# A graph network's filter layer: one-hots compared with a row of numbers in PSUM, place sums read in neighbouring order

## The reference

```python
h = x @ w_in + b_in
Wij = ssp(f_ij @ w_f1 + b_f1) @ w_f2 + b_f2      # ssp = softplus - log 2
Wij = Wij * rcut_ij[:, None]                     # one row of 64 per edge
x_ij = h[idx_j] * Wij
agg = jax.ops.segment_sum(x_ij, idx_i, num_segments=n_atoms)
out = ssp(agg @ w_o1 + b_o1) @ w_o2 + b_o2
```

## Time and profile before

| what | us |
|---|---|
| median of 3 runs | 7495.95 |
| lowest and highest | 7493.87, 7500.98 |
| the profiled execution | 7511.49 |
| its span in the profile | 7509.8 |

### The profile page before, as it was taken

One profiled execution on the slowest core, in us unless ns is written; L12 is line 12 of the kernel. 1 busy time (PEld: TensorE's weight loads), 2 busy tenths in 40 slices (PEclk: granted clock), 3 DMA queues, 4 the chain that ended last, 5 costly groups with the idle time before them and its releaser, 6 DMA issues. The chain is left out here.

```text
span 7509.8 us, 155131 instructions
## 1 busy us (share of the span) xinstructions
PE 5888.8 (78%) x41800; PEld 4261.6 (57%) x41800; DVE 5381.3 (72%) x14198; ACT 3602.2 (48%) x5657; POOL 5249.8 (70%) x5375
## 2 busy tenths in 40 slices
PE   7777777777777888878777774666999999999994
PEld 6555555555555666666555553554666666666662
DVE  7766767677677888888888884445777777777774
ACT  2555555555555555555555552044333333333334
POOL 4677777777777777777777775534777777777770
PEclk5666666666666667676667776677999999999995
DMA  4222222111113333333333335744222222222222
GB/s 127 79 83 82 84 84 69 55 56 54 55 55 89 111 114 115 110 118 94 93 96 93 93 89 157 248 133 152 77 76 76 77 77 77 76 76 76 76 77 74
DMA packets 512098, 695.12 MB, mean 93 GB/s; under 512 B 255299, under 2 KB 367645, under 8 KB 510879
## 3 DMA queue, kind: packets, MB, share of 16 engines
q1 hardware_dynamic: 317008, 347.69, 16.3%
q0 software_dynamic: 181376, 321.40, 14.5%
q10 hardware_dynamic: 13498, 24.07, 1.0%
HBM read 450.80 MB, written 241.85 MB: 92 GB/s over the span
## 5 line engine op out<-in xcount | busy, mean ns | idle before, releaser
L1688 POOL DMA_INDIRECT msg_tab<-big x3224 | 3318.4, 1029 | 1076.3 <-issue 1076.0
L2239 POOL DMA_INDIRECT big<-y_parts,big x1616 | 1589.2, 983 | 547.7 <-issue 485.5
L2320 ACT CAST big<-ps 128x980 bf16<-128x980 f32 x804 | 783.9, 975 | 1272.3 <-PE ps L2268 1269.6
L2280 PE MATMUL ps<-big 128*128 128x384 bf16 x6566 | 1196.4, 326 | 0.2 <-ACT big L2320 0.2
L2372 DVE TENSOR_SCALAR big<-big,dstF 128x343 bf16<-128x343 f16 (+2 forms) x3216 | 981.9, 338 | 238.5 <-PE ps L2268 235.5
L1187 PEld LDWEIGHTS ps<-big 128*128 128x128 f32 x3224 | 651.4, 300 | 432.9 <-ACT big L1376 432.9
L1187 PE MATMUL ps<-big 128*128 128x128 f32 x3224 | 764.0, 412 | 154.6 <-ACT big L1376 154.6
L1381 ACT CAST big<-big 128x512 bf16<-128x512 f32 x403 | 249.2, 618 | 1213.4 <-DMA msg_tab<-big 1213.0
L1491 DVE TENSOR_TENSOR big<-big 128x512 f32<-128x512 f32 x403 | 279.2, 693 | 762.6 <-ACT big L1381 759.9
L2280 PEld LDWEIGHTS ps<-big 128*128 128x128 bf16 x6566 | 580.5, 97 | 347.9 <-issue 1.0
L1487 DVE TENSOR_REDUCE big<-big 128x8 f32<-128x784 f32 x403 | 637.7, 1582 | 13.7
(11 more groups left out here) (289 smaller groups left out, 10740.7 us busy)
## 6 DMA issues: line engine op xcount, KB each, us to landing
arena<-msg_tab SPq DMA_DIRECT2D x97, 727.5 KB, 4.6
big<-msg_tab SPq DMA_DIRECT2D x97, 630.5 KB, 4.1
big<-in_edge_attr SPq DMA_DIRECT2D x403, 128.0 KB
msg_tab<-big POOLq DMA_INDIRECT x3224
big<-msg_tab SPq DMA_DIRECT2D x97, 388.0 KB, 3.4
msg_tab<-big SPq DMA_DIRECT2D x97, 291.0 KB
big<-y_parts,big POOLq DMA_INDIRECT x1616
big<-h_parts SPq DMA_DIRECT2D x403, 48.0 KB
```

The source lines that it names most:

```text
L1688: nc.gpsimd.indirect_dma_start(out=m.msg_tab[:, :], out_offset=bass.IndirectOffsetOnAxis(ap=sidx[s][:, j:j + 1], axis=0), in_=row[s][:, j, ...
L2239: nc.gpsimd.indirect_dma_start(out=m.grow[s][:, 3 * D * j:3 * D * j + 3 * D], out_offset=None, in_=m.y_parts[:, :], in_offset=bass.Indirec ...
L2280: mm = pe.matmul(ps_rows, m.cnt[h][:, a, :], m.y_part[:, HALF * h + a, :], start=(h == 0 and a == 0), stop=(h == 1 and a == HALF - 1))
L2320: nc.scalar.copy(m.cnt[h][:, :, SLOTS * i:SLOTS * i + SLOTS].rearrange("p h (a w) -> p h a w", a=2), ps_cnt[i % 2][:, :, 0:SIDE * HALF].re ...
```

## The change

- The bf16 table `digit` goes. Instead VectorE copies the numbers 0 to 127 once as fp32 into PSUM (`ps_count`, in the bank that also holds `ps_rank`), and L1477 compares against that row, each number repeated by a step of zero.
- `hot_seg`'s compare (L1531) reads `ps_count` too, instead of `node_early`. It moves from the end of the stage to right behind L1477, ahead of the sum L1481.
- `prod` now lies edge by edge (p, j, h): L1485 writes at a step of 98 words, L1487 reads neighbouring words.
- The wait for `total_made` moves ahead of the first compare, since PE writes `ps_rank` in the same bank; PE waits for the tables before it zeroes `ps_rank`.

```diff
@@ -860,8 +860,7 @@
     row = [v.bitcast(BF16).rearrange("p (j c) -> p j c", j=J) for v in slots(8176, J * MROW // 2)]
     far = work[:, 9728:10240].bitcast(BF16)
     tile_hot = m.spare[:, 0:NBK]
-    prod = work[:, 10240:10240 + NBK * J].rearrange("p (h j) -> p h j", j=J)
-    digit = work[:, 11024:11024 + NBK * J // 2].bitcast(BF16).rearrange("p (h j) -> p h j", j=J)
+    prod = work[:, 10240:10240 + NBK * J].rearrange("p (j h) -> p j h", j=J)
     lower = work[:, 11416:11544]
     sidx = [v.bitcast(U32) for v in slots(11544, J)]
     rank = slots(11560, J)
@@ -921,6 +920,7 @@
     ps_row = ps[:, 3, :]
     ps_rank = ps[:, 4, 0:NBK]
     ps_attr = ps[:, 5, 0:2 * P]
+    ps_count = ps[:, 4, P:2 * P]
     ps_dst = ps[:, 6:8, :].rearrange("p a b -> p (a b)")
     ps_bucket = [ps[:, t, 0:3 * F] for t in range(3)]
     e_ps_attr = ps[:, 1, 0:2 * P]
@@ -1249,8 +1249,8 @@
             pe.sem_inc(total_made, 1)
             pe.sem_inc(deg_turned, 2)
             pe.sem_inc(bucket_summed, 3)
+            pe.wait_ge(tables_put, 4)
             pe.matmul(ps_rank, m.zeros[0:1, 0:P], m.zeros[0:1, 0:NBK], start=True, stop=False, skip_group_check=True)
-            pe.wait_ge(tables_put, 4)
             pe.sem_inc(seg_summed, 1)
             staged_parts(pe, G, stage)
 
@@ -1458,7 +1458,7 @@
             dve.wait_ge(weighed_done, ready(g, 1))
 
         def dve_windows(dve):
-            nc.vector.tensor_copy(digit, m.iota_w[:, 0:NBK].unsqueeze(2).to_broadcast([P, NBK, J])).then_inc(tables_put, 1)
+            nc.vector.tensor_copy(ps_count, m.iota_w[:, :]).then_inc(tables_put, 1)
             nc.vector.tensor_scalar(lower, m.below[:, :], -1.0, 1.0, ALU.mult, ALU.add).then_inc(tables_put, 1)
             for s in range(2):
                 nc.vector.memset(row[s][:, :, MROW - 1:MROW], 0.0).then_inc(tables_put, 1)
@@ -1473,18 +1473,20 @@
                 dve.wait_ge(low_done, free(g))
                 nc.vector.tensor_tensor(msg, ps_row, weighed, ALU.mult).then_inc(msg_done, 1)
 
-            def rank_hots(g):
-                nc.vector.tensor_tensor(hot, digit, m.hi16[:, bass.ds(g * J, J)].unsqueeze(1).to_broadcast([P, NBK, J]),
+            def rank_hots(g, part):
+                dve.wait_ge(total_made, free(g))
+                nc.vector.tensor_tensor(hot, ps_count[:, 0:NBK].unsqueeze(2).to_broadcast([P, NBK, J]), m.hi16[:, bass.ds(g * J, J)].unsqueeze(1).to_broadcast([P, NBK, J]),
                                         ALU.is_equal).then_inc(hot_done, 1)
+                if part and not (isinstance(part[1], int) and part[1] == NBK - 1):
+                    hot_seg(*part)
                 dve.wait_ge(hot_done, ready(g, 0))
-                dve.wait_ge(total_made, free(g))
                 nc.vector.tensor_reduce(tile_hot, hot, AX.X, ALU.add).then_inc(hots_added, 1)
 
             def ranks(g, s):
                 dve.wait_ge(prefix_made, ready(g, 0))
-                nc.vector.tensor_tensor(prod, hot, ps_rank.unsqueeze(2).to_broadcast([P, NBK, J]), ALU.mult).then_inc(rank_mul, 1)
+                nc.vector.tensor_tensor(prod.rearrange("p j h -> p h j"), hot, ps_rank.unsqueeze(2).to_broadcast([P, NBK, J]), ALU.mult).then_inc(rank_mul, 1)
                 dve.wait_ge(rank_mul, ready(g, 0))
-                nc.vector.tensor_reduce(rank[s], prod.rearrange("p h j -> p j h"), AX.X, ALU.add).then_inc(rank_done, 1)
+                nc.vector.tensor_reduce(rank[s], prod, AX.X, ALU.add).then_inc(rank_done, 1)
 
             def rest(g, s):
                 dve.wait_ge(high_done, ready(g, 0))
@@ -1528,7 +1530,8 @@
                 nc.vector.tensor_copy(seg_low[:, 0:n], seg[s][:, 0:n, 3 * F]).then_inc(seg_lows, 1)
                 dve.wait_ge(seg_lows, q + 1)
                 dve.wait_ge(seg_summed, q + 1)
-                nc.vector.tensor_tensor(seg_hot[:, 0:P * n].rearrange("p (n r) -> p n r", r=n), node_early[:, :, 0:n],
+                nc.vector.tensor_tensor(seg_hot[:, 0:P * n].rearrange("p (n r) -> p n r", r=n),
+                                        ps_count.unsqueeze(2).to_broadcast([P, P, n]),
                                         seg_low[:, 0:n].unsqueeze(1).to_broadcast([P, P, n]), ALU.is_equal).then_inc(seg_hots, 1)
 
             def seg_loads(phase, s, k):
@@ -1541,7 +1544,7 @@
                 if before:
                     message(*before[:2])
                 if here:
-                    rank_hots(here[0])
+                    rank_hots(here[0], (*part, slot_of(part, here)) if part else None)
                 if part and not (isinstance(part[1], int) and part[1] == 0):
                     fold_seg(part[0], part[1] - 1, slot_of(part, here) ^ 1)
                 if before:
@@ -1554,8 +1557,6 @@
                     places(*before[:2])
                 if after:
                     dve_hidden(dve, after[0], hid[after[1]], relu, log1p)
-                if part and not (isinstance(part[1], int) and part[1] == NBK - 1):
-                    hot_seg(part[0], part[1], slot_of(part, here))
             for t in range(2):
                 dve.sem_inc(parts_out[t], 16)
             dve.sem_inc(seg_folded, 1)
```

## The result

The kernel with the change takes 7525.53 us (median of 6 runs, 7518.53 to 7531.95), the kernel before 7498.47 us (6 runs, 7482.70 to 7503.00): a ratio of 1.0038, 95% interval 1.0025 to 1.0051. It is slower by some 27 us, where 38 were forecast. The profiled execution took 7525.14 us, its span 7523.4 us. The spans differ by only 13.6 us (7509.8 before), since the profiled execution of before lay 13 us above the median of its runs and that of after on its median.

What follows compares the result with a forecast made beforehand. In the first band VectorE's 10.29 us barely exceeds GpSimd's bare 10.15, and whichever has more to do sets the turn. First band +36 us, second +2, without buckets 0: +38 us, median 7534 us, 8-in-10 range 7450 to 7590.

Steps and rivals of the forecast that it cites:

- The side: Whole kernel: slower, chance 0.60, against 0.20 for the same and 0.20 for faster.
- VectorE's sum sets the first band: First band with buckets: VectorE's turn becomes 10.29 + 0.41 + 0.79 - 0.01 = 11.48 us, over 11.11 us.
- Every price of an instruction: VectorE: place compare about 0.96 us, node compare 1.9 and 1.2, product 1.55, sum over buckets 0.97.
- The two halves of the sums cancel: L1485 and L1487: sum -0.61 us by neighbouring reads, product +0.60 by its strided store, together -0.01 us.
- The turns without buckets hide all of it: Turns without buckets: VectorE's 3.1 us of slack hide +0.40 us, so 0.
- the strided store: L1485's store at 98 words: +0.60 us taken, bounds 0 and +0.61; the quoted skill figure would give 1.14 us.
- First band: The 98 turns of the first band with buckets: +0.37 us each, +36 us in all.
- Nothing on the path gains by that … Both cost nothing: Moved node compare and wait for total_made: PE's 3.85 us of idle goes, but both were priced at nothing.
- Second band: The 97 turns of the second band: VectorE 10.81 us against 10.86; 0 to +0.1 us taken, +2 us in all.
- GpSimd's own time stays near 10.8 as well, since the stretches at L1498 stay: Second band: GpSimd's turn not shortened by the change, the ground for taking 0 to +0.1 us.
- GpSimd is freed: Rival, L1531 and L1477: without two SBUF operands their stretches end, both bands 10.65 us, -65 us, 7431 us; chance 0.07.
- GpSimd meets L1498: Rival, turns without buckets: L1498 over about 0.1 us earlier stretches a DMA instruction, +80 us, about 7610 us; chance 0.10.

Runs made afterwards that it cites:

- old_sums: The changed kernel with prod back in its old order, dense product store and strided sum over buckets: 7524.58 us, ratio to before 1.0028.
- node_sbuf: The changed kernel with the node compare reading the old bf16 table in SBUF again, at its new place: 7441.12 us, ratio to before 0.9920.
- no_move: The changed kernel with the node one-hot back at the end of VectorE's stage, plus a wait for total_made: 7613.14 us, ratio to before 1.0160.
- move_only: The kernel before with only the node one-hot moved behind the place one-hot, both tables in SBUF: 7464.89 us, ratio to before 0.9952.
- place_psum: The kernel before with only the place compare changed to read the row in PSUM: 7474.34 us, ratio to before 0.9982.
- place_row_sbuf: The kernel with the bf16 node compare (node_sbuf), its place compare reading the fp32 row from SBUF instead of PSUM: 7506.56 us, ratio to before 1.0021.
- row_in_sbuf: The changed kernel with both compares reading the same fp32 row from SBUF instead of PSUM: 7552.35 us, ratio to before 1.0081.
- sum_later: The kernel before with the sum over buckets L1487 moved behind the low part L1498: 7574.76 us, ratio to before 1.0108.
- low_first: The kernel before with L1495 (0.2 us) moved behind L1498, which so comes about 0.1 us earlier: 7526.97 us, ratio to before 1.0034.
- hidden_later: node_sbuf with the hidden sum L1452 moved into the next stage, between L1456 and L1474: 7424.91 us, ratio to before 0.9911.
- hidden_move: move_only with the hidden sum L1452 moved between L1456 and L1474: 7487.41 us, ratio to before 0.9999.

## Why the prediction was right, and where not

**Right, and shown.** The side: slower, by 27 us where 38 were forecast, 7525.5 us in the forecast's own range. VectorE's sum sets the first band: 11.48 us forecast, 11.43 on the timeline, with GpSimd behind L1505. Every price of an instruction: 0.96, 1.9 and 1.2, 1.55, and 0.97 us were forecast for what took 0.963, 1.891, 1.224, 1.575 and 0.970. The two halves of the sums cancel (old_sums). The turns without buckets hide all of it (10.65 and 10.63). And the repeated fp32 row is what costs: node_sbuf gets 84 us back by a bf16 table.

On the strided store the trace stood nearer to my bounds than to the figure I had quoted. The product went from 966 to 1575 ns, 0.78 ns an element. The 1.14 us estimated from the Trainium skill's 24-word step (Vector Engine (DVE) Microarchitecture Reference, "Measured stream behaviour on trn2") did not come; the same table has 1.75 ns a column for reads at 72 and 152 words, and that is the row which the 98-word store is like, with 1.044 + 0.78 = 1.82.

**First band, mis-sized: +25 us for +36.** The steady turn was near the forecast. From one of GpSimd's pauses to the next 14 turns take 11.41 us each, and the last four turns of the band only 10.53, 10.50, 10.48 and 10.18: VectorE starts its last compare of 1664 elements at 3441 us, 40 us before GpSimd is through with the band. So 11.37 us is the mean. The sum took the steady turn for all 98.

**The step that failed: "Nothing on the path gains by that … Both cost nothing".** The move is worth 40 us by itself, and undoing it in the change costs 88, of which some 40 are the old place and 48 the wait in the shared bank. The sum had nothing for it. I took two turns of the timeline in which VectorE waits for nothing as the band. The row of L1485 in the earlier trace rows has 49.2 us of waiting for PE's L1212, and 44.9 of these lie in 45 turns of the first band. They belong to a loop: node one-hot last on VectorE, 3.85 us of PE idle, counts late, VectorE late. Where VectorE sets the pace, as in the change, such a wait adds to the turn (0.34 us in no_move). In the kernel before GpSimd sets it, and there the move pays by GpSimd's stretch, 0.82 to 0.43 us a turn. The forecast of +36 us for the band was still fair, but by luck: its sum began from VectorE's own 10.29 us, in which no wait stands, and so had the gain in it without knowing.

As parts, in the order in which the kernels can be lined up on one chip: move -40 us (before to move_only), place compare in PSUM with the new sums -24 us (to node_sbuf), node compare with the fp32 row +83 us (to old_sums, with the old sums), +20 us in all. The place compare alone in the kernel before is -15 us, so the parts depend on what else is in the kernel, and a sum of parts from different kernels proves little, however near it comes to the 27 us.

**Second band, probably of the wrong sign: -0.13 us for "0 to +0.1".** The 12 us are no more than the 13 that can't be placed. The step was "GpSimd's own time stays near 10.8 as well, since the stretches at L1498 stay". GpSimd's stretch fell from 0.55 to 0.43 us a turn, and it moved: in instructions that start within L1498 (L1500 with the change) from 0.28 to 0.05, within L1531 (L1533) from 0.11 to nothing, within the place compare from 0.06 to nothing, and within L1491 (L1493) it rose from 0.08 to 0.32. VectorE's own sum, 10.81 us in the forecast, is 10.65, and with 0.09 us of waiting for ACT it makes the 10.73.

Three kernels say what the parts do here. The move alone gives -0.09 us. The row in PSUM gives -0.33 where VectorE's turn is shorter (place_psum), and +0.48 comes back with the row in SBUF (place_row_sbuf). But in the change itself it gives next to nothing: with the rows in SBUF (row_in_sbuf) the band takes 10.76 us for 10.73. The rival "GpSimd is freed" so held a part of the truth: its mechanism is there, but where VectorE is the later one it only changes stretch into waiting, as row_in_sbuf shows in the first band (11.37 and 11.39 us with .05 and 1.14 of stretch). It gives time back only where GpSimd sets the pace.

**The rival "GpSimd meets L1498"** had the right kind of mechanism (sum_later is 80 us of it) and a wrong edge: 0.1 us was not enough (low_first), and the phase of all eight instructions moves with any edit, so that one meeting is no unit to price.

**Open.** The 13 us between spans and medians. Why the stretch falls with the move alone. Whether the fp32 type or the repeat makes the compares long. Why hidden_later gains and hidden_move loses. What GpSimd's pause of 2 us every 14 turns is.

## What to carry to other kernels

Before a step is priced at nothing, read the idle column of the consumers' rows over the whole band, not two turns of the timeline: a wait in half of the turns is invisible in a lucky pair. Then ask who sets the pace: where it is VectorE, its waits add to the turn, and where it is GpSimd, only GpSimd's stretches do. What an operand is and where it lies are two prices: the repeated fp32 row lengthens VectorE's compare wherever it lies, and one operand in PSUM frees GpSimd, which pays only where GpSimd sets the pace. The best of both here was to put the short compare in PSUM, to leave the long one in bf16, and to build what another engine waits for early in the stage (node_sbuf, 0.992).

## What the runs showed of the hardware

- GpSimd's indirect DMA instruction is held by a VectorE instruction with two SBUF operands until 0.83 to 0.85 us behind that instruction's end: behind L1531, L1493, L1500, L1491 and L1478 alike. In 21 cases before it is held until 0.84 us behind the small bf16 copy L1528 as well, which has one operand. On GpSimd's side only the start counts: in the fourteen traces together, VectorE's instructions of 512 elements with two SBUF operands take 0.73 us in the median (400 of 440 over 0.70) when they start between 0.03 us ahead of and 0.01 us behind a start of GpSimd's. They take 0.68 (all but one of 6790 at most 0.71) when they start 0.05 to 0.6 us behind it. With one operand in PSUM they take 0.68 in the first case too (85 of 85 under 0.69).
- If it starts 0.01 us behind VectorE it goes through in 0.97 us (low_first, 74 of 74), at 0.04 us it takes 1.48 (sum_later); at 0.03 and 0.04 us either happens (6 of 9 and 6 of 7 stretched in low_first).
- A compare of 784 elements with one fp32 row takes 963 ns with the row in PSUM and 965 ns in SBUF, and 557 ns with bf16 operands only, the table stored out in full.
- PE's granted clock in the first band, where the move removed its waits for L1531, is 0.77 after (2368 to 3481 us) for 0.68 before. It is the move that does it: in the stretch from 2368 to 3458 us move_only has 0.77 too, and no_move 0.68. In the change it is worth nothing, since PE then waited 242.1 us for VectorE ahead of L1212. The window of after (its length, busy us and instructions of PE, PEld, DVE, ACT and POOL, the granted clock as a share of full speed, the share of the DMA engines, GB/s) and the wait:

```profile
2368.00:3481.00 1113.00, 820.52 (x6253) 633.79 (x6252) 1027.40 (x1662) 605.32 (x981) 762.96 (x784) 0.77 0.38 110
```

```profile
PE ps L1212 <- DVE big L1483: 242.1, 98, 3.0
```
